# A decoder layer with its self-attention fed from a host-transposed x, the normalisation folded in later, and a new instruction order

## The chip, the core and the metric

The kernel runs on one core of one Trainium2 chip. The metric is the device time of one execution in microseconds; the engines named are PE (TensorE), DVE (VectorE), ACT (ScalarE), POOL (GpSimd) and SP (SyncE, which here only issues DMAs).

## The reference

One decoder layer on 8 items of 512 tokens and 256 channels, in f32:

```python
x = x + attn(layernorm(x))          # one head of 128: q, k, v = xn @ w_q, xn @ w_k, xn @ w_v
                                    # softmax(q k^T / sqrt(128)) v, times head_dim_mask, @ w_o
x = x + xattn(layernorm(x), ctx)    # relu(xn W^T + b), relu(ctx W^T + b), masked softmax, times ctx
x = x + ffn(layernorm(x))           # ternary weights, activations rounded to 8 bits per token:
                                    # silu(gate) * up, 1024 wide, then down to 256
```

`layernorm` subtracts the mean over the 256 channels and divides by sqrt(var + 1e-5); it has no weights.

## The kernel before

The work is cut into streams. Stream A is the self-attention of an item, E projects the item's context, B is the cross-attention, C the feed-forward part, W prepares the weights. A step is written `A.S2/3`: stream A, step S2, item 3. Five lists written out in the file (`PE_ORDER`, `ACT_ORDER`, `DVE_ORDER`, `POOL_ORDER`, `SP_ORDER`) fix what each engine runs, one entry after the other; semaphores join the engines. An engine whose next entry isn't ready waits, and everything behind it in its list waits too. All DMAs are issued by SP, in the order of its list.

Products are made in f32r from a high and a low part: `product3` (L821 to L823) issues high by high, low by high, high by low. So each operand needs a high part (ACT copies it with rounding) and a low part (a subtraction on DVE, or on POOL).

Stream A of one item, as it stands: `bn` and `ag` (DVE) give mean and variance of each token, `rs` (POOL, L537 and L539) gives 1/std, `sh` (DVE, L1040) gives -mean/std, and `norm` (ACT, L632) writes the normalised rows `a_xn`. XT0 and XT1 transpose them on PE (L847), eight 128x128 blocks in all. ACT rounds the two halves from PSUM into `a_xT_hi` (L645), DVE subtracts into `a_xT_lo` (L1139). V, Q and K are products of 6 matmuls each, 512 columns wide. ACT copies V out (L649), PE transposes it (VT). S0 to S3 are the four row blocks of the scores, 3 matmuls each; DVE takes each one's row maximum (L1144), ACT the exponential straight from PSUM (L657) into one of two halves of `a_p`; P0 to P3 transpose that on PE (L878). H is the product with v, 12 matmuls, and Y0, Y1 the product with `w_o`, 12 matmuls half as wide, which DVE adds to x.

Item 0 alone uses five PSUM banks for stream A; later items alternate between two. The start holds the first items' loads (SP), the splitting of all weights, and W.sum0 to W.sum5 (DVE, L1220), the sums of the feed-forward weights, of which sum2 and sum3 need `w_up`. E.YP0 and E.YP1 of an item are 6 matmuls each.

The stretch from the warm-up matmuls (L995) to item 1 reads in `PE_ORDER`:

```python
    A.XT0/0 A.XT1/0 E.YP0/0 A.V/0 A.Q/0 A.K/0 A.VT/0 E.YP1/0 A.S0/0 A.S1/0 A.S2/0 A.S3/0 A.P0/0 A.P1/0 A.P2/0
    A.P3/0 E.YP0/1 A.H/0 E.YP1/1 A.Y0/0 A.Y1/0 W.total/0 A.XT0/1 A.XT1/1 E.YP0/2 A.V/1 A.Q/1 A.K/1 B.XT0/0
```

Of the kernel before, what the change touches and what calls it, by code (L numbers as in the profile page):

```python
# [36 lines left out]
A_LO = ["XT0", "XT1", "Q", "K", "VT", "P0", "P1", "P2", "P3", "H"]  # L37
# [151 lines left out]
    S.hT3/6 S.xqT3/7 S.hT0/7 S.store/6 S.hT1/7 S.hT2/7 S.hT3/7 S.store/7""".split()  # L189


def decoder_layer(nc, x, ctx, ctx_t, mask, head_mask, w_qkv, w_o, W, b, w_gate, w_up, w_down, out):
    B, S = mask.shape
    D, DH = w_o.shape[1], w_o.shape[0]
    F = w_gate.shape[2]
# [1128 lines left out]
```

## Time and profile before

| | us |
|---|---|
| median of 3 runs | 399.21 |
| lowest, highest | 398.03, 399.86 |
| the profiled execution, its own time | 398.97 |
| its span (first to last instruction) | 397.2 |

The profiled execution lies 0.24 us under the median, and 1.8 us lie outside its span. The profile says how long each engine was busy and what ended its idle times. In a row of a timeline the first number is the start, the second the duration; matmuls are pipelined, so their starts tell their pace, not their durations.

### The profile page before, as it was taken

How to read it: one execution, taken by the hardware profiler on the slowest of the kernel's cores; microseconds unless marked ns; L12 is line 12 of the kernel's file. 1: busy time of each engine (PE TensorE's matmuls, PEld its weight loads, DVE VectorE, ACT ScalarE, POOL GpSimd, SP SyncE). 2: the span in 40 equal slices, each digit the busy share in tenths (PEclk: the TensorE clock that was granted, in tenths of full speed). 3: DMA queues.
4: the chain of work that ended last, by engine and by line, in shares of the span. 5: the costliest groups of instructions: out<-in, count | busy, mean ns of one | idle time of the engine just before them, and what ended most of it. 6: DMA issues, size and time to landing. Idle time of an engine off the chain costs nothing.

```text
span 397.2 us, 7277 instructions
## 1 busy us (share of the span) xinstructions
PE 372.9 (94%) x2158; PEld 289.4 (73%) x2158; DVE 332.4 (84%) x908; ACT 328.1 (83%) x611; POOL 270.3 (68%) x398
## 2 busy tenths in 40 slices
PE   5889989999999999999999999999999999999673
PEld 5666667877797688777787778877887788578332
DVE  2999745958998799888998599988997989899991
ACT  3696997699979887998797998889989978966861
POOL 3466931298779846998588786888568866974540
PEclk9699999999999999999999999999999999999995
DMA  7951100022133421225241342252203001432364
GB/s 228 414 196 55 54 2 1 9 66 66 29 59 94 144 57 35 60 61 173 33 71 58 94 127 28 41 141 66 49 6 94 14 0 30 121 65 54 101 139 106
DMA packets 50087, 32.18 MB, mean 81 GB/s; under 512 B 43649, under 2 KB 45313, under 8 KB 49665
## 3 DMA queue, kind: packets, MB, share of 16 engines
q1 hardware_dynamic: 50048, 31.73, 30.1%
q8 instruction: 17, 0.28, 0.3%
q14 instruction: 22, 0.17, 0.2%
HBM read 17.04 MB, written 4.19 MB: 53 GB/s over the span
## 4 chain that ended last, share of the span: by engine, by line
PE 49%; DVE 15%; ACT 14%; issue 10%; POOL 7%; DMA 3%; SPq 1%; DVEq 0%; POOLq 0%; ACTq 0%
PE b_bank L821 5%; PE b_bank L823 5%; PE b_bank L822 5%; PE d_bank L990 4%; PE u_bank L981 4%; PE g_bank L981 4%; PE a_bank L821 3%; PE a_bank L823 3%; PE a_bank L822 3%; POOL c_work L547 2%; PE a_bank L878 2%; DVE h_max L1201 2%; PE b_bank L940 2%; PE e_bank L821 2%; DMA hm_i<-in_head_mask 2%
## 5 line engine op out<-in xcount | busy, mean ns | idle before, releaser
L547 POOL TENSOR_TENSOR c_work<-c_work 128x512 f32<-128x512 f32 x48 | 61.9, 1291 | 20.4 <-DVE c_work L1189 13.2
L588 POOL TENSOR_SCALAR c_work<-c_work,h_q 128x1024 f32<-128x1024 f32 x32 | 36.1, 1128 | 19.6 <-DVE h_q L1208 19.6
L990 PE MATMUL d_bank<-downT,c_half 128*128 128x256 bf16 x256 | 34.9, 282 | 9.0 <-DMA c_half<-c_half 5.4
L750 ACT ACTIVATE c_half<-c_work 128x1024 bf16<-128x1024 f32 x32 | 33.8, 1056 | 9.5 <-POOL c_work L588 9.4
L1201 DVE TENSOR_REDUCE h_max<-c_work 128x1 f32<-128x1024 f32 x32 | 38.8, 1212 | 2.4 <-POOL c_work L547 2.1
L740 ACT ACTIVATE c_work<-g_bank,c_tanh_scale 128x512 f32<-128x512 f32 x52 | 36.4, 699 | 4.2 <-PE g_bank L981 3.1
L821 PE MATMUL b_bank<-ctx_hi,b_pT_hi 128*128 128x256 f32 x128 | 38.9, 304 | 0.0
L1189 DVE SCALAR_TENSOR_TENSOR c_work<-c_work,g_bank 128x512 f32<-128x512 f32 x52 | 35.4, 680 | 3.7 <-ACT c_work L740 3.0
L990 PEld LDWEIGHTS d_bank<-downT,c_half 128*128 128x128 bf16 x256 | 24.4, 100 | 19.1 <-DMA c_half<-c_half 8.3
L822 PE MATMUL b_bank<-ctx_lo,b_pT_hi 128*128 128x256 f32 x128 | 36.1, 282 | 0.0
L823 PE MATMUL b_bank<-ctx_hi,b_pT_lo 128*128 128x256 f32 x128 | 36.1, 282 | 0.0
L981 PE MATMUL g_bank<-gateT,xqT 128*128 128x512 bf16 x112 | 33.5, 381 | 1.2 <-ACT c_work L728 0.9
L981 PE MATMUL u_bank<-upT,xqT 128*128 128x512 bf16 x112 | 33.6, 382 | 0.2 <-DMA xqT<-xq 0.2
L743 ACT ACTIVATE c_work<-u_bank 128x512 f32<-128x512 f32 x48 | 29.2, 609 | 4.6 <-PE u_bank L981 2.8
L1144 DVE TENSOR_REDUCE a_nmax<-a_bank 128x1 f32<-128x512 f32 x29 | 19.9, 687 | 14.7 <-PE a_bank L823 14.5
L514 POOL TENSOR_TENSOR yp_lo<-e_relu,yp_hi 128x512 fp32r<-128x512 f32 x16 | 20.7, 1293 | 14.1 <-ACT yp_hi L677 14.1
L821 PE MATMUL b_bank<-yp_hi,xp_hi 128*128 128x512 f32 x64 | 28.4, 444 | 0.0
L686 ACT ACTIVATE b_p<-b_p,b_nmax 128x512 f32<-128x512 f32 x32 | 23.6, 736 | 3.3 <-DVE b_nmax L1169 3.3
L821 PEld LDWEIGHTS b_bank<-ctx_hi,b_pT_hi 128*128 128x128 f32 x128 | 24.3, 190 | 2.0 <-DVE b_pT_lo L1163 0.6
L823 PE MATMUL b_bank<-yp_hi,xp_lo 128*128 128x512 f32 x64 | 25.2, 394 | 0.0
L822 PE MATMUL b_bank<-yp_lo,xp_hi 128*128 128x512 f32 x64 | 25.1, 392 | 0.0
L822 PEld LDWEIGHTS b_bank<-ctx_lo,b_pT_hi 128*128 128x128 f32 x128 | 24.3, 190 | 0.4
(254 smaller groups left out, 1278.4 us busy)
## 6 DMA issues: line engine op xcount, KB each, us to landing
ctxT_raw<-in_ctx_t SPq DMA_DIRECT2D x8, 512.0 KB, 3.9
ctx_raw<-in_ctx SPq DMA_DIRECT2D x8, 512.0 KB, 3.5
x_all<-in_x SPq DMA_DIRECT2D x7, 512.0 KB, 3.8
out<-x_all SPq DMA_DIRECT2D x7, 512.0 KB, 2.6
c_half<-in_w_down SPq DMA_DIRECT2D x1, 1024.0 KB, 7.4
c_work<-in_w_gate SPq DMA_DIRECT2D x1, 1024.0 KB, 10.1
c_work<-in_w_up SPq DMA_DIRECT2D x1, 1024.0 KB, 11.7
x_all<-in_x SPq DMA_DIRECT2D x2, 256.0 KB, 2.8
```

The lines of the kernel that those rows point to most:

```text
L547: pool.tensor_tensor(h[:, t % 2, half * HALF:(half + 1) * HALF], th[:, j % 2, :], up[:, j % 2, :], ALU.mult).then_inc(hs, 1)
L588: pool.tensor_scalar(h[:, t % 2, :], h[:, t % 2, :], h_q[:, t:t + 1], ROUND, ALU.mult, ALU.add).then_inc(h_rounds, 1)
L740: act.activation(th[:, j % 2, :], gu_bank("g", j, n), ACT.Tanh, scale=c_tanh_scale[:, j // 2:j // 2 + 1]).then_inc(tanhs, 1)
L743: act.activation(up[:, j % 2, :], gu_bank("u", j, n), ACT.Copy).then_inc(ups, 1)
L750: act.activation(h_q8[:, t % 2, :], h[:, t % 2, :], ACT.Copy, bias=-ROUND).then_inc(hqs, 1)
L821: pe.matmul(dst, l_hi, r_hi, start=first, stop=False)
L822: pe.matmul(dst, l_hi, r_lo, start=False, stop=False)
L823: return pe.matmul(dst, l_lo, r_hi, start=False, stop=last)
L981: mm = pe.matmul(dst, xqT[:, t * DC + c, :], w[:, c, cols], start=c == 0, stop=c == DC - 1)
L990: mm = pe.matmul(d_bank[:, 0:D], h_T[:, t % 2, f, :], downT[:, f, :], start=f == 0, stop=f == FC - 1)
L1189: dve.scalar_tensor_tensor(th[:, j % 2, :], th[:, j % 2, :], 1.0, gu_bank("g", j, n), ALU.add, ALU.mult).then_inc(gates, 1)
L1201: dve.tensor_reduce(h_max[:, one], h[:, t % 2, :], AX.X, ALU.max, apply_absolute_value=True).then_inc(h_maxes, 1)
```

## The change

x is loaded twice: as rows, for the residual and the statistics, and as `x_t`, transposed on the host (`a_xT_raw`, 512 KB an item). Attention works on the raw x. Taking the mean off the channels of x is the same as taking the mean over the 256 channels off each column of the weights, so `w_qkv` is centred once (W.colsum on PE, W.centre on DVE). 1/std is a factor of a token: of a column of v and of a column of the scores it enters by a row `r_bc` of 512 values, the same in all partitions; of a row of the scores it enters as a scalar. `r_bc` is made by two DMAs an item: S.rw stores 1/std to a row in DRAM, S.rb reads it back broadcast to 128 partitions. So that the row comes out in order, tokens are numbered 4 to a partition, and q is written with its columns re-ordered.

XT0, XT1, `norm`, `sh` and the copy of V are gone. In their place stand `xT0`, `xT1` (ACT rounds from SBUF; the low part is made by POOL, for item 0 by DVE), the product of V with `r_bc` on DVE, and for each S one DVE operation that multiplies, writes `a_p` and takes the maximum, with a small one behind it that negates the maximum. ACT's exponential now reads `a_p`. The bank of an S is free again once DVE has read it; before, once ACT had taken the exponential. As DVE now writes `a_p`, S2 and S3 wait on DVE for P0 and P1.

All five lists are new.

```diff
+            def load_xT(n):
+                if n > 1:
+                    sp.wait_ge(xT_loaded, (n - 1) * 16)
+                    sp.wait_ge(xT_split, DC * (n - 1))
+                else:
+                    sp.wait_ge(xT0_split, DC)
+                sp.dma_start(a_xT_raw[:, :, :], x_t[:, n]).then_inc(xT_loaded, 16)
...
+            def store_r(n):
+                sp.wait_ge(a_rstds, 4 * n + 4)
...
+                sp.dma_start(r_rows[n, :].rearrange("(p t) -> p t", t=T), a_rstd[:, n % 2, :]).then_inc(r_stored, 16)
...
+            def load_r(n):
+                sp.wait_ge(r_stored, 16 * n + 16)
...
+                    sp.wait_ge(a_maxed, T * n)
+                sp.dma_start(r_bc[:, :], r_rows[n, :].partition_broadcast(P)).then_inc(r_loaded, 16)
...
+            def xT_rest(c, n):
+                pool.wait_ge(xT_his, DC * n + c + 1)
+                pool.tensor_tensor(a_xT_lo[:, c, :], a_xT_raw[:, c, :], f32(a_xT_hi[:, c, :]), ALU.subtract).then_inc(xT_split, 1)
...
-            def copy_v(n):
-                act.wait_ge(a_filled, a_rank("V", n))
-                act.activation(vT[:, :], a_bank("V", n)[:, :], ACT.Copy).then_inc(vT_copied, 1)
...
+            def round_xT(c, n):
...
+                act.activation(a_xT_hi[:, c, :], a_xT_raw[:, c, :], ACT.Copy).then_inc(xT_his, 1)
...
-                act.wait_ge(a_maxed, T * n + t + 1)
...
-                act.activation(a_p[:, t % 2, :], a_bank(f"S{t}", n)[:, :], ACT.Exp,
+                act.wait_ge(a_nmaxes, T * n + t + 1)
+                act.activation(a_p[:, t % 2, :], a_p[:, t % 2, :], ACT.Exp,
...
-                    for t in range(T):
-                        if c == 0 and t % 2 == 0:
-                            pe.wait_ge(a_xns, 2 * n + t // 2 + 1)
-                        mm = pe.transpose(dst[:, t * P:(t + 1) * P], a_xn[:, t, c * P:(c + 1) * P], ident[:, :])
...
+                if name == "colsum":
+                    pe.wait_ge(qkvo_loaded, 16)
+                    for c in range(DC):
+                        mm = pe.matmul(b1_bank[:, 0:3 * DH], ones[:, :], wqkv_raw[:, c, :, :].rearrange("p w d -> p (w d)"),
+                                       start=c == 0, stop=c == DC - 1)
...
-                    dve.tensor_reduce(a_nmax[:, t:t + 1], src[:, :], AX.X, ALU.max, negate=True).then_inc(a_maxed, 1)
+                    if t > 1:
+                        dve.wait_ge(a_filled, a_rank(f"P{t - 2}", n))
...
+                    dve.tensor_tensor_reduce(a_p[:, t % 2, :], src[:, :], r_bc[:, :], a_rstd[:, n % 2, t:t + 1], MASKED, ALU.mult, ALU.max,
+                                             a_max[:, t:t + 1]).then_inc(a_maxed, 1)
+                    dve.wait_ge(a_maxed, k)
+                    dve.tensor_scalar(a_nmax[:, t:t + 1], a_max[:, t:t + 1], -1.0, None, ALU.mult).then_inc(a_nmaxes, 1)
+                elif step == "V":
+                    dve.wait_ge(a_filled, a_rank(step, n))
+                    dve.wait_ge(r_loaded, 16 * n + 16)
+                    dve.tensor_tensor(vT[:, :], src[:, :], r_bc[:, :], ALU.mult).then_inc(vT_copied, 1)
...
+            def centre_qkv():
+                dve.wait_ge(qkv_sums, 1)
+                for c in range(DC):
...
+                    last = dve.scalar_tensor_tensor(raw, b1_bank[:, 0:3 * DH], -1.0 / D, raw, ALU.mult, ALU.add)
+                last.then_inc(qkv_centred, 1)
```

Of `PE_ORDER` the piece that answers to the one above now reads:

```diff
+    W.colsum/0 A.Q/0 A.K/0 A.V/0 A.VT/0 A.S0/0 A.S1/0 A.S2/0 A.S3/0 A.P0/0 A.P1/0 E.YP0/0 A.P2/0 A.P3/0 E.YP1/0
+    W.total/0 A.H/0 E.YP0/1 A.Y0/0 A.Y1/0 E.YP1/1 A.Q/1 A.K/1 A.V/1 A.VT/1 B.XT0/0 B.XT1/0 A.S0/1 A.S1/1 B.XP0/0
```

SP's list at the start, of before; `in_w_qkv` and `in_w_o` go to `b_p`, `in_w_up` and `in_w_gate` to `c_work`:

```order
L452 DMA x_all<-in_x 128x512 x2
L409 DMA ctxT_raw<-in_ctx_t 128x1024
L456 DMA b_p<-in_w_qkv 128x768
L458 DMA b_p<-in_w_o 128x256
L460 DMA bias<-in_b 128x2
L462 DMA hm_i<-in_head_mask 128x1
L454 DMA xqT<-in_W 128x512
L465 DMA c_half<-in_w_down 128x2048
L397 DMA x_all<-in_x 128x1024
L465 DMA c_work<-in_w_gate 128x2048
L416 DMA mask_u<-in_mask 128x512
L465 DMA c_work<-in_w_up 128x2048
```

And of the changed kernel, the piece from the fifth load on; `r_rows` is the row in DRAM, `r_bc` its broadcast:

```order
L406 DMA x_all<-in_x 128x1024
L498 DMA c_work<-in_w_gate 128x2048
L439 DMA ctxT_raw<-in_ctx_t 128x1024
L412 DMA ctx_raw<-in_ctx 128x1024
L498 DMA c_half<-in_w_down 128x2048
L446 DMA mask_u<-in_mask 128x512
L495 DMA hm_i<-in_head_mask 128x1
L498 DMA c_work<-in_w_up 128x2048
L426 DMA r_rows<-a_rstd 128x4
L406 DMA x_all<-in_x 128x1024
L420 DMA a_xT_raw<-in_x_t 128x1024
L433 DMA r_bc<-r_rows 128x512
```

Ahead of this piece stand x (two halves), `w_qkv`, the bias, `x_t` (two halves), W and `w_o`. What moved: `x_t` of item 0 and the contexts now stand in front of `w_up`, and the store of 1/std stands behind `w_up`, its broadcast read two loads of 512 KB further on.

DVE's list of before from the splitting of `w_o` (W.wo, L1242 to L1245) to W.sum2; L1251 splits W, L1220 is a W.sum:

```order
L1242 CAST hm_f<-hm_i 128x1
L1243 TENSOR_SCALAR b_p<-b_p,hm_f 128x256
L1244 CAST wo_hi<-b_p 128x256
L1245 TENSOR_TENSOR wo_lo<-b_p,wo_hi 128x256
L1247 TENSOR_TENSOR wqkv_lo<-b_p,wqkv_hi 128x768
L1251 TENSOR_TENSOR wt_lo<-xqT,wt_hi 128x512
L1139 TENSOR_TENSOR a_xT_lo<-a_bank,a_xT_hi 128x512 x2
L1028 BN_STATS a_bn<-x_all 128x6 x4
L1035 BN_AGGR a_mv<-a_bn 128x2 x4
L1220 TENSOR_REDUCE w_sum<-c_work 128x1
L1040 TENSOR_SCALAR a_shift<-a_mv,a_rstd 128x1 x2
L1220 TENSOR_REDUCE w_sum<-c_work 128x1 x2
```

And of the changed kernel from W.sum0 on; L1214 is the product of V with `r_bc`, L1323 belongs to W.wo, the splitting of `w_o`, and L1207 with L1210 to the step S:

```order
L1290 TENSOR_REDUCE w_sum<-c_work 128x1 x2
L1188 SCALAR_TENSOR_TENSOR q_lo<-a_bank,q_hi 128x512
L1290 TENSOR_REDUCE w_sum<-c_work 128x1
L1196 TENSOR_TENSOR k_lo<-a_bank,k_hi 128x512
L1214 TENSOR_TENSOR vT<-g_bank,r_bc 128x512
L1322 CAST hm_f<-hm_i 128x1
L1323 TENSOR_SCALAR b_p<-b_p,hm_f 128x256
L1324 CAST wo_hi<-b_p 128x256
L1325 TENSOR_TENSOR wo_lo<-b_p,wo_hi 128x256
L1196 TENSOR_TENSOR v_lo<-u_bank,v_hi 128x512
L1207 ISA a_p,a_max<-d_bank,r_bc,a_rstd 128x512
L1207 ISA a_max 128x1
```

What moved: W.wo and the split of W (L1329) stood ahead of item 0's scores and of everything that waits for a load of `w_up`; now W.wo stands behind the product with `r_bc`, the split of W behind S1. Behind the piece follow S2, S3, P0, P1, three of the six sums, P2, P3, the statistics of items 1 to 3, W.scales and H.

## Rows read from the trace of the kernel before

**Rows 1.** The page: busy us, share of the span and instructions of each engine
```profile
PE 372.9 (94%) x2158; PEld 289.4 (73%) x2158; DVE 332.4 (84%) x908; ACT 328.1 (83%) x611; POOL 270.3 (68%) x398
```

**Rows 2.** Busy by stretch: stretch, length, PE, PEld, DVE, ACT, POOL, clock, DMA share, GB/s
```profile
10.00:20.00 10.00, 8.53 (x29) 6.50 (x30) 9.51 (x20) 6.75 (x13) 4.23 (x6) 0.66 1.01 415
20.00:30.00 10.00, 8.75 (x47) 6.65 (x46) 9.40 (x15) 9.49 (x20) 6.00 (x4) 1.00 0.54 189
30.00:40.00 10.00, 9.05 (x48) 6.84 (x47) 9.47 (x34) 6.81 (x13) 6.32 (x7) 1.00 0.19 55
50.00:60.00 10.00, 8.62 (x46) 7.00 (x45) 4.83 (x10) 10.00 (x19) 2.82 (x3) 1.00 0.01 2
100.00:140.00 40.00, 39.96 (x246) 32.05 (x245) 35.09 (x93) 35.71 (x68) 32.50 (x45) 1.00 0.34 88
```

**Rows 3.** What PE waited for: us in total, times, longest us
```profile
PE d_bank L990 <- DMA c_half<-c_half: 5.4, 4, 2.7
PE a_bank L847 <- ACT a_xn L632: 3.9, 2, 3.6
```

**Rows 4.** Timeline of PE: start us, us, engine, line, operation, count, idle before
```profile
20.80 0.60 PE L863 MATMUL a_bank<-ident,vT 128*128 128x128 f32 x4
...
21.70 0.40 PE L823 MATMUL e_bank<-ctxT_hi,wt_lo 128*128 128x512 f32 x1
21.94 0.39 PE L821 MATMUL e_bank<-ctxT_hi,wt_hi 128*128 128x512 f32 x1
...
37.50 1.44 PE L847 MATMUL a_bank<-ident,a_xn 128*128 128x128 f32 x8 [0.17 <-DVE x_all L1151]
...
246.25 1.03 PE L847 MATMUL a_bank<-ident,a_xn 128*128 128x128 f32 x8
247.12 0.59 PE L981 MATMUL u_bank<-upT,xqT 128*128 128x512 bf16 x2
```

**Rows 5.** Groups of instructions: line, engine, operation, count, busy us, mean ns, idle
```profile
L847 PE MATMUL a_bank<-ident,a_xn 128*128 128x128 f32 x64 | 10.5, 296 | 4.2 <-ACT a_xn L632 3.9 <-DVE x_all L1151 0.2
...
L1169 DVE CUSTOM_DVE_ANT_0 b_p<-b_bank,mask_add 128x512 f32<-128x512 f32 x32 | 21.9, 683 | 0.9 <-PE b_bank L823 0.8
...
L1028 DVE BATCH_NORM_STATS2 a_bn<-x_all 128x6 f32<-128x256 f32 x32 | 11.6, 412 | 3.4 <-DMA x_all<-in_x 3.4
...
L1139 DVE TENSOR_TENSOR a_xT_lo<-a_bank,a_xT_hi 128x512 fp32r<-128x512 f32 x16 | 10.4, 681 | 0.2 <-ACT a_xT_hi L645 0.2
...
L1040 DVE TENSOR_SCALAR a_shift<-a_mv,a_rstd 128x1 f32<-128x1 f32 x32 | 5.2, 206 | 2.2 <-POOL a_rstd L539 2.2
...
L632 ACT ACTIVATE a_xn<-x_all,a_shift,a_rstd 128x256 f32<-128x256 f32 x32 | 17.1, 594 | 1.9 <-DVE a_shift L1040 1.9
...
L514 POOL TENSOR_TENSOR yp_lo<-e_relu,yp_hi 128x512 fp32r<-128x512 f32 x16 | 20.7, 1293 | 14.1 <-ACT yp_hi L677 14.1
```

**Rows 6.** Timelines of POOL (first row) and DVE, 5 to 30 us
```profile
8.90 2.35 POOL L510 TENSOR_TENSOR ctxT_lo<-ctxT_raw,ctxT_hi 128x1024 fp32r<-128x1024 f32 x1 [1.74 <-ACT ctxT_hi L707]
...
9.80 1.59 DVE L1243 TENSOR_SCALAR b_p<-b_p,hm_f 128x256 f32<-128x256 f32 x1
11.43 0.29 DVE L1244 CAST wo_hi<-b_p 128x256 fp32r<-128x256 f32 x1
11.76 0.43 DVE L1245 TENSOR_TENSOR wo_lo<-b_p,wo_hi 128x256 fp32r<-128x256 f32 x1
...
19.36 1.22 DVE L1220 TENSOR_REDUCE w_sum<-c_work 128x1 f32<-128x1024 f32 x1 [0.42 <-DMA c_work<-in_w_up]
...
25.75 0.68 DVE L1144 TENSOR_REDUCE a_nmax<-d_bank 128x1 f32<-128x512 f32 x1
26.35 1.21 DVE L1220 TENSOR_REDUCE w_sum<-c_half 128x1 f32<-128x1024 f32 x1
```

**Rows 7.** DMA issues: out<-in, queue, count, KB each, median us to landing
```profile
c_work<-in_w_up SPq DMA_DIRECT2D x1, 1024.0 KB, 11.7
...
mask_u<-in_mask SPq DMA_DIRECT2D x8, 64.0 KB, 3.2
```

More of the change, by code:

```diff
@@ L192, in decoder_layer @@
-def decoder_layer(nc, x, ctx, ctx_t, mask, head_mask, w_qkv, w_o, W, b, w_gate, w_up, w_down, out):
+    W.colsum/0 A.Q/0 A.K/0 A.V/0 A.VT/0 A.S0/0 A.S1/0 A.S2/0 A.S3/0 A.P0/0 A.P1/0 E.YP0/0 A.P2/0 A.P3/0 E.YP1/0
+    W.total/0 A.H/0 E.YP0/1 A.Y0/0 A.Y1/0 E.YP1/1 A.Q/1 A.K/1 A.V/1 A.VT/1 B.XT0/0 B.XT1/0 A.S0/1 A.S1/1 B.XP0/0
+    B.XP1/0 A.P0/1 A.S2/1 E.YP0/2 A.P1/1 A.S3/1 B.S0/0 B.S1/0 A.P2/1 A.P3/1 B.P0/0 B.S2/0 A.H/1 B.P1/0 B.O0/0
+    A.Y0/1 B.S3/0 B.P2/0 A.Y1/1 A.Q/2 B.O1/0 B.P3/0 A.K/2 B.O2/0 B.O3/0 A.V/2 B.XT0/1 B.XT1/1 E.YP1/2 A.VT/2
@@ L193, in decoder_layer @@
+def decoder_layer(nc, x, x_t, ctx, ctx_t, mask, head_mask, w_qkv, w_o, W, b, w_gate, w_up, w_down, out):
     B, S = mask.shape
@@ L1029, in a_norm @@
                     last.then_inc(a_stats, 1)
-                elif part == "ag":
+                else:
                     dve.wait_ge(a_stats, k)
                     if n > 0:
-                        dve.wait_ge(a_shifts, k - 2)
+                        dve.wait_ge(a_rstds, 2 * (k - 2))
                     for t in pair(half):
@@ L1036, in a_norm, with xT0_rest @@
                     last.then_inc(a_mvs, 1)
-                else:
-                    dve.wait_ge(a_rstds, 2 * k)
-                    for t in pair(half):
-                        last = dve.tensor_scalar(a_shift[:, t:t + 1], a_mv[:, t, 0:1], a_rstd[:, t:t + 1], -1.0, ALU.mult, ALU.mult)
-                    last.then_inc(a_shifts, 1)
+            def xT0_rest(c):
+                dve.wait_ge(xT_his, c + 1)
+                dve.tensor_tensor(a_xT_lo[:, c, :], a_xT_raw[:, c, :], f32(a_xT_hi[:, c, :]), ALU.subtract).then_inc(xT0_split, 1)
             def b_norm(part, half, n):
@@ L1258, in step @@
                     else:
-                        {"split": split_qkvo, "lo": split_W, "scales": prep_scales}[name]()
+                        {"centre": centre_qkv, "split": split_qkv, "wo": split_wo, "lo": split_W, "scales": prep_scales}[name]()
+                elif name[:2] == "xT":
+                    xT0_rest(int(name[2]))
                 elif name[:2] in ("ag", "sh") and stream == "C" and n == LAST:
@@ L1300 @@
     laid_out = {
-        "x": tokens(x),
+        "x": own_tokens(x),
+        "x_t": x.reshape(*x.shape[:2], -1, P).transpose(3, 0, 2, 1),
         "ctx": tokens(ctx),
```

449 lines of the change are left out of this document (243 added, 206 removed).

## The prediction

> **What bounds the kernel now.** I read the page's busy shares first. PE is busy for 372.9 of 397.2 us, DVE 84%, ACT 83%, POOL 68% [rows 1]. The reader is to see one engine nearly full and none far below it. Then the table of stretches, since a share is a mean: from 100 to 140 PE has 39.96 of 40 us, with DVE at 35.09, ACT at 35.71 and POOL at 32.50 [rows 2]. There PE is the bound. In the first 40 us it isn't: PE has 8.53, 8.75 and 9.05 of each 10 while DVE has 9.51, 9.40 and 9.47, so DVE is the fuller one; and DMA is saturated from 10 to 20 (share 1.01, 415 GB/s) [rows 2]. Last the list of what PE waited for: 5.4 us for the transposed h, at the end of the kernel, and 3.9 us for the normalised x, nearly all of it in one wait of 3.6 at the start [rows 3]. So the change must be judged twice: where PE is full, and in the start.
>
> **PE in the full part.** 64 transposes go [rows 5]. Their mean duration of 296 ns is not their price, since they overlap: eight of them start at 246.25 and the next work at 247.12, so 0.11 us each [rows 4]. For items 1 to 7 that is 56 x 0.11 = 6.2 us off PE. As PE is full there, I count all of it. It is the only gain that reaches the end.
>
> **The other engines in the full part.** DVE loses 16 subtractions (10.4 us) and 32 shifts (5.2 us) [rows 5]. It gains 8 products with `r_bc` and 32 small negations, and the 32 row maxima become multiply-and-maximum operations. A PSUM-reading operation of 128x512 takes 0.68 to 0.69 whichever it is: L1139 681 ns, L1169, which is the same kind as the new one, 683 ns [rows 5], the old maximum 0.68 [rows 6]. So the maxima cost the same, the products 8 x 0.68 = 5.5, the negations 32 x 0.21 = 6.6 at the price of L1040 [rows 5], and 32 reads of an accumulator some 0.1 each, 3: together 15.1 against 15.6. DVE stands as it was. ACT loses the norms, 17.1 us [rows 5], and the copies of V; that is hidden by PE. POOL gains 14 subtractions at 1.293 us [rows 5], 18 us in all, 2.6 an item: from 32.5 to about 35 in a stretch of 40 [rows 2]. That is hidden by PE too, as long as POOL's latencies don't grow; if that cover goes, 2.6 us an item are the most it can cost. The pair of DMAs for 1/std holds SP: when S.rb stands right behind S.rw, SP stands still until the row is stored, about the 3.2 us of a small load [rows 7], and the transposes of h stand behind it. PE waited for those only at the end [rows 3], so I count nothing.
>
> **The start.** Here the order decides. First the loads. The store of 1/std stands behind `w_up`. Before, `w_up` landed at 19.4: DVE's sum waited for it until 19.36 [rows 6]. By the shapes in the two lists (128x1024 in f32 are 512 KB; the mask is 64 KB) before has 5,441 KB up to and with `w_up`, the new list 6,465 KB, since `ctx` and the 512 KB of `x_t` now stand in front of it. 1,024 KB at 415 GB/s [rows 2] are 2.5 us: `w_up` lands at 21.9, and the row of 1/std hardly before, because a small DMA doesn't overtake: `w_up` needed 11.7 us although it is only 1,024 KB, which alone is 2.5 us [rows 7]. The read of `r_bc` is issued then, behind 1,024 KB more and with 256 KB of its own: 3.1 us, 25.0. An idle queue would give 21.9 + 3.2 = 25.1 [rows 7], so both ways lead to the same time. Until 25.0 DVE stands at the product of V, and behind it stands all that it does for item 0.
>
> Then the work behind that wait. DVE's list from A.V/0 up to H of item 0 has: 8 operations of 128x512, 0.60 apart (25.75 to 26.35) [rows 6], 4.8; 4 steps S at 0.60 + 0.1 + 0.21, 3.6; W.wo, from 9.80 to 12.19 in before [rows 6] and a small cast, 2.5; three sums of 1.21 that overlap by 0.1 [rows 6], 3.3; 6 statistics at 0.41 [rows 5], 2.5; 21 small ones (aggregations, a reciprocal, W.scales), which I put at 0.12 each, under L1040's 0.206 because they overlap, 2.5. Together 19.2. So H's low part is ready at 44.2. Y0 and Y1 (12 half-wide matmuls, 1.4) and E.YP1/1 (6 at 0.24 [rows 4], 1.4) follow, and A.Q/1 starts at 47.0. Before, the same place in the work is 37.50 plus eight transposes, 38.4 [rows 4]: by then both kernels have done four YP steps and item 0's attention. **The delay is 8.6 us.**
>
> Its bounds. If DVE were no limit, PE would need from 25.7 on: 48 matmuls at 0.24, 20 transposes at 0.11, 12 half-wide at 0.12, 15.1 us [rows 4], so A.Q/1 at 40.8 and a delay of 2.4. From above, some 2 us of waits of ACT and POOL between DVE's operations, 10.6. I take 8.6, because DVE's operations in this stretch stood back to back in before (9.40 and 9.47 of 10 [rows 2]) and work that used to lie before 24 us (W.wo, the split of W, W.sum3) is now behind 25. The new matmuls of W.colsum fall while PE has nothing else, and item 0's own transposes are within the delay as counted.
>
> W.wo has a price that hangs on its neighbour. Its multiplication took 1.59 us, while a cast of the same shape took 0.29, and POOL's L510 ran from 8.90 to 11.25 beside it [rows 6]. In the new order POOL's two `a_xT_lo` of item 1 fall beside it again, so I keep 2.5. The Trainium skill (SBUF — State Buffer, SBUF: two separate sides) says that DVE and GpSimd arbitrate for one pair of ports, "an exclusive lock, not a bandwidth split". By that rule, W.wo without POOL beside it would be 1.2, the delay 7.3 and the whole 400.1; the rule and the row agree on the collision, and what it leaves open is only whether POOL is there.
>
> **The sum**, against the profiled execution's own time: 398.97 - 6.2 + 8.6 = 401.4. That execution lies 0.24 below the median, so 401.6, which I round to **401.5 us**, 0.6% slower. A measurement of this kernel tells about 0.5%, 2.0 us, from no change.
>
> **Rivals.**
> - *The delay is made good later; faster.* Between 50 and 60 PE had only 8.62 and ACT all of 10 us [rows 2]. ACT loses four norms an item, 2.1 us; for items 1 and 2, 4.2, and PE's idle 1.4 of that stretch could be filled. 401.4 - 5.6 = 395.8. For it: DVE has room there (4.83 of 10). Against it: PE can only work off what it waits for, and it waits little after 60. It decides once the place of A.S0/2 in the new trace is less than 4 us late. 0.27.
> - *The row of 1/std comes sooner; no change.* If a small DMA does overtake the loads, V's product still waits for W.sum2, which needs `w_up`: 21.9 + 1.1 + 0.6 for K, 23.6 rather than 25.0, and with W.wo free of POOL another 1.3 less. 401.4 - 1.4 - 1.3 = 398.7. Against it: 11.7 us for `w_up`. 0.16.
> - *POOL and SP lose as well; clearly slower.* If the 2.6 us that POOL gets more an item show on the path at only a quarter, seven items cost 4.5: 405.9. For it: POOL is at 81% in the full part. 0.17.
> - *The forecast*, start late, transposes saved: 0.40, its own range 399.5 to 404.
>
> **The numbers.** The forecast's own 0.40 splits at 401.2, the bound of 0.5%, into 0.25 above and 0.15 below. Slower: 0.25 + 0.17 = 0.42. Within 0.5%: 0.15 + 0.13 of the second rival + 0.02 of the first, 0.30. Faster: 0.25 + 0.03, 0.28. The range takes the delay's lower bound, 398.97 - 6.2 + 2.4 = 395.2, at one end, and the third rival at the other: 395 to 406.
>
> **What would show it.** In the new trace: V's product on DVE ends an idle time near 25 with a DMA as releaser; A.VT/0 near 25.8 against 20.80; H of item 0 around 41 to 45 on PE; A.Q/1 near 47. In the full part eight transposes fewer per item, PE still at 39.9 of 40, POOL near 35. It is wrong if `r_bc` lands before 22, if DVE idles between 25 and 44, if PE idles visibly more than before between 60 and 340, or if PE's waits at the end, 5.4 for h [rows 3], change by more than 2 us, which the new order could do and the trace of before can't tell.

## The result, and the profile after

The changed kernel takes **405.21 us** (median of four runs, 403.0 to 406.9) against 399.19 for the kernel before: a ratio of 1.015, 95% interval 1.0086 to 1.0215, 6.0 us slower. The profiled execution was its fastest run: 403.0 us with a span of 401.2. It is 4.0 us above the profiled execution of before, where the forecast was 2.4.

Two rows of the page of the changed kernel, its span and the busy share of each engine, to be read beside [rows 1]:

```profile
span 401.2 us, 7242 instructions
...
PE 367.7 (92%) x2098; PEld 283.6 (71%) x2098; DVE 331.2 (83%) x936; ACT 311.4 (78%) x571; POOL 287.3 (72%) x412
```

PE has 5.2 us less, ACT 16.7 less, POOL 17.0 more, DVE the same within 1.2: near the counts of the prediction (6.2 off PE, 17.1 and the copies of V off ACT, 18 on POOL, DVE as it was). The table of stretches (columns as in [rows 2]) says where the time went:

```profile
10.00:20.00 10.00, 6.01 (x18) 4.48 (x18) 5.31 (x8) 1.20 (x2) 0.00 (x0) 0.83 0.85 342
20.00:30.00 10.00, 3.27 (x10) 2.79 (x11) 5.72 (x9) 3.21 (x5) 2.99 (x3) 0.60 0.52 192
30.00:40.00 10.00, 8.01 (x37) 6.00 (x36) 9.69 (x25) 8.04 (x17) 6.42 (x7) 0.88 0.59 177
40.00:50.00 10.00, 7.35 (x36) 5.88 (x37) 9.36 (x31) 6.00 (x8) 8.54 (x6) 1.00 0.40 104
...
100.00:140.00 40.00, 40.00 (x236) 31.86 (x236) 35.91 (x104) 34.15 (x66) 33.38 (x48) 1.00 0.27 62
```

From 10 to 30 us PE has 9.3 us of work where it had 17.3 [rows 2], and DVE, which was nearly full, 11.0 of 20. From 100 on PE is full as before. The rest is in four timelines of the changed kernel. First DVE (start us, us, engine, line, operation, idle before it and who ended it):

```profile
22.17 1.22 DVE L1290 TENSOR_REDUCE w_sum<-c_work 128x1 f32<-128x1024 f32 x1 [6.05 <-DMA c_work<-in_w_up]
...
25.99 0.69 DVE L1214 TENSOR_TENSOR vT<-g_bank,r_bc 128x512 f32<-128x512 f32 x1 [2.00 <-DMA r_bc<-r_rows]
26.78 1.26 DVE L1323 TENSOR_SCALAR b_p<-b_p,hm_f 128x256 f32<-128x256 f32 x1
...
41.99 1.25 DVE L1297 TENSOR_TENSOR w_mean<-w_half 128x3 f32<-128x3 f32 x1
43.28 1.23 DVE L1298 TENSOR_SCALAR w_mean<-w_mean 128x3 f32<-128x3 f32 x1
44.54 0.18 DVE L1299 RECIPROCAL w_inv<-w_mean 128x3 f32<-128x3 f32 x1
...
46.36 0.67 DVE L1196 TENSOR_TENSOR hT_lo<-g_bank,hT_hi 128x512 fp32r<-128x512 f32 x1
```

Then SP's queue, with the store of 1/std and its broadcast; POOL beside DVE's two slow tiny operations; and PE:

```profile
9.15 0.56 SPq L426 DMA_DIRECT2D r_rows<-a_rstd  x1
...
22.68 0.33 SPq L433 DMA_DIRECT2D r_bc<-r_rows  x1
```

```profile
40.82 2.40 POOL L553 TENSOR_TENSOR ctxT_lo<-ctxT_raw,ctxT_hi 128x1024 fp32r<-128x1024 f32 x1
43.18 1.31 POOL L557 TENSOR_TENSOR yp_lo<-e_relu,yp_hi 128x512 fp32r<-128x512 f32 x1
```

```profile
26.73 1.12 PE L915 MATMUL u_bank<-ident,vT 128*128 128x128 f32 x4 [8.89 <-DVE vT L1214]
...
28.50 0.63 PE L881 MATMUL d_bank<-k_hi,q_lo 128*128 128x512 f32 x1
28.93 0.63 PE L879 MATMUL a_bank<-k_hi,q_hi 128*128 128x512 f32 x1
...
47.14 0.36 PE L879 MATMUL u_bank<-wo_hi,hT_hi 128*128 128x256 f32 x1 [2.19 <-DVE hT_lo L1196]
...
50.03 0.39 PE L879 MATMUL a_bank<-a_xT_hi,wqkv_hi 128*128 128x512 f32 x1
```

The reader is to see one chain. The store of 1/std, 2 KB, was issued at 9.15, but SP, which waits for that store to land, could issue the broadcast only at 22.68, half a us after `w_up` had landed. So V's product stands at 25.99, PE idles 8.89 us in one piece, and all of item 0 follows late. The last row is A.Q/1, the first work of item 1. In the kernel before, the same place in the work is the end of item 1's eight transposes, 38.4 ([rows 4], as in the prediction); its first product of item 1 itself starts at 40.78, behind one product of E. In the changed kernel the place is 50.03. **11.6 us are lost up to there.** From there to the end of the span before needed 358.8 us and the changed kernel 351.2. **7.6 us are given back.** The difference is the 4.0. What the 7.6 are made of stands in the table of stretches, taken from that place to the end, before and then changed:

```profile
38.40:397.20 358.80, 342.19 (x2018) 264.82 (x2018) 302.78 (x833) 303.02 (x567) 251.49 (x369) 0.99 0.27 65
```

```profile
50.03:401.20 351.17, 336.76 (x1967) 259.05 (x1965) 296.80 (x854) 289.33 (x536) 266.57 (x383) 0.99 0.33 78
```

PE is busy for 5.4 us less and idle for 2.2 us less (14.4 and not 16.6).

This pair, where A.Q/1 starts and what is left from there, is what the experiments are measured by.

### The profile page after: what moved, and what is told of

Its sections match the earlier page's. It is cut to its first block, busy times and chain, and to the rows that moved or that the text cites. A ratio compares the mean times of both kernels' runs of the same rounds, so it can differ in the third digit from the quotient of the medians.

```text
span 401.2 us, 7242 instructions
## 1 busy us (share of the span) xinstructions
PE 367.7 (92%) x2098; PEld 283.6 (71%) x2098; DVE 331.2 (83%) x936; ACT 311.4 (78%) x571; POOL 287.3 (72%) x412
## 4 chain that ended last, share of the span: by engine, by line
PE 55%; POOL 14%; DVE 9%; issue 7%; DMA 7%; ACT 6%; SPq 2%; POOLq 0%; ACTq 0%; DVEq 0%
PE b_bank L879 7%; PE b_bank L881 7%; PE b_bank L880 7%; PE a_bank L879 4%; PE a_bank L881 4%; PE a_bank L880 4%; PE g_bank L1033 4%; PE u_bank L1033 3%; DMA r_rows<-a_rstd 3%; PE d_bank L1042 3%; POOL c_work L601 3%; PE b_bank L992 3%; PE a_bank L926 2%; POOL c_work L642 2%; DMA c_half<-c_half 2%
## 5 line engine op out<-in xcount | busy, mean ns | idle before, releaser
L549 POOL TENSOR_TENSOR a_xT_lo<-a_xT_raw,a_xT_hi 128x512 fp32r<-128x512 f32 x14 | 17.9, 1294 | 18.1 <-ACT a_xT_hi L715 18.1
L1207 DVE CUSTOM_DVE_ANT_0 a_p<-a_bank,r_bc,a_rstd 128x512 f32<-128x512 f32 x30 | 22.4, 746 | 8.3 <-PE a_bank L881 8.1
L879 PE MATMUL b_bank<-yp_hi,xp_hi 128*128 128x512 f32 x64 | 27.4, 428 | 0.2
L545 POOL TENSOR_TENSOR ctx_lo<-ctx_raw,ctx_hi 128x1024 fp32r<-128x1024 f32 x8 | 19.2, 2398 | 10.6 <-ACT ctx_hi L762 10.6
L719 ACT ACTIVATE a_p<-a_p,a_nmax 128x512 f32<-128x512 f32 x32 | 23.7, 745 | 3.6 <-DVE a_nmax L1210 3.6
```

The lines of the kernel that those rows point to most:

```text
L879: pe.matmul(dst, l_hi, r_hi, start=first, stop=False)
```

## The experiments

| kernel | median us | ratio to before | A.Q/1 at | from there on |
|---|---|---|---|---|
| changed kernel | 405.2 | 1.015 (1.009 to 1.022) | 50.03 | 351.2 |
| row early | 407.2 | 1.021 (1.018 to 1.023) | 54.05 | 352.0 |
| row early, path clear | 402.6 | 1.009 (1.006 to 1.012) | 47.79 | 352.0 |
| DVE cleared | 405.6 | 1.016 (1.014 to 1.019) | 51.58 | 351.9 |
| both | 399.5 | 1.003 (1.000 to 1.006) | 43.91 | 353.2 |
| transposes back | 408.8 | 1.026 (1.022 to 1.029) | 53.16 | 355.3 |
| POOL twice | 420.1 | 1.053 (1.049 to 1.056) | 51.45 | 364.2 |
| scales later | 409.3 | 1.028 (1.025 to 1.031) | 48.95 | 357.6 |
| start reordered | 412.4 | 1.034 (1.031 to 1.037) | 50.11 | 360.4 |
| POOL a quarter | 404.9 | 1.014 (1.010 to 1.018) | 53.57 | 350.7 |
| ACT twice | 410.5 | 1.028 (1.025 to 1.032) | 53.01 | 356.1 |
| second order | 407.3 | 1.021 (1.017 to 1.024) | 42.95 | 361.8 |
| third order | **397.4** | **0.9976 (0.9958 to 0.9995)** | 38.43 | 355.8 |

The last two columns are those of the profiled run. The fourth is not sharp: between runs with the same lists up to there it differs by up to 3.5 us, and 1.5 of these are PE's clock (see "DVE cleared"). All medians of before in these comparisons lie between 398.8 and 399.2.

### Is it the row of 1/std?

**Row early.** SP's list alone is changed:

```diff
-S.x/1 W.gate/0 S.ctxT/0 S.ctx/0 W.down/0 S.mask/0 W.hm/0 W.up/0 S.rw/0 S.x/2 S.xT/1 S.rb/0
+S.x/1 S.rw/0 W.gate/0 S.ctxT/0 S.rb/0 S.ctx/0 W.down/0 S.mask/0 W.hm/0 W.up/0 S.x/2 S.xT/1
```

> The changed kernel, with only the two DMAs of item 0's 1/std row moved forward in SP's list: the store right behind x of item 1, the broadcast read right behind the context. Theory 1 (the row waits behind the loads of w_up and w_down, and that is what starts item 0's scores late): the row lands near 14.5 instead of 26, but V's product still stands behind W.sum2 on DVE, which needs w_up near 22; so V's product moves from 26.0 to about 24.5, PE's wait at A.VT/0 shrinks by 1.5, and the time falls by 1.5 us, to about 403.5 by the median. Rival (the path of item 0 doesn't matter, the loss is spread over the items): nothing moves by more than 0.5 us.

It was slower than the changed kernel. In DVE's timeline the row isn't waited for any more, but the sum that stands ahead of the product comes 3.2 us later:

```profile
25.34 1.22 DVE L1290 TENSOR_REDUCE w_sum<-c_work 128x1 f32<-128x1024 f32 x1 [7.00 <-DMA c_work<-in_w_up]
...
27.07 0.68 DVE L1214 TENSOR_TENSOR vT<-g_bank,r_bc 128x512 f32<-128x512 f32 x1
```

SP stands still until 1/std is there and again until it is stored, and every load behind it is issued later. `w_up` was issued at 13.28 and not at 8.65. In the changed kernel DVE had waited only 2.00 us for the row, so more than that was not to be had from the row alone, and SP's wait took it away again. A.Q/1 moved by 4.0 us and V's product by 1.1; 1.5 of the difference is PE's clock, granted at 0.50 from 50 to 52 us, as told under "DVE cleared".

**Row early, path clear.** The same, with DVE's W.sum2, which needs `w_up`, behind A.S1/0, and ACT's and POOL's rounding of item 1's x behind A.exp1/0 and E.ctxT/0:

```diff
 DVE
-A.Q/0 W.sum2/0 A.K/0 A.V/0 W.wo/0 A.VT/0 A.S0/0 A.S1/0 W.lo/0
+A.Q/0 A.K/0 A.V/0 W.wo/0 A.VT/0 A.S0/0 A.S1/0 W.sum2/0 W.lo/0
```

> As e1_row_early, and the steps that stand in front of item 0's path and wait for late loads are moved behind it: W.sum2 on DVE (needs w_up) behind A.S1/0, the rounding of item 1's x on ACT behind A.exp1/0, and its low part on POOL behind E.ctxT/0. Theory 1: V's product near 18.5 instead of 26.0, A.VT/0 near 19.5, A.Q/1 near 43 instead of 50.0, and the time 7 us lower, about 398 by the median. Rival A (DVE's own list, not the wait, sets A.Q/1): A.Q/1 moves by less than 3 us, time near 403. Rival B (the loss is spread over the items): time as the changed kernel's.

V's product came at 18.62, 7.4 us earlier. A.Q/1 came only 2.2 us earlier, and the median fell by 2.6, which is the size that rival A had. From V's product to the end of H's low part it now took 26.2 us and not 21.0. DVE's next step wanted a load that hadn't come either:

```profile
22.74 0.15 DVE L1320 CAST hm_f<-hm_i 128x1 f32<-128x1 int32 x1 [3.44 <-DMA hm_i<-in_head_mask]
22.93 1.62 DVE L1321 TENSOR_SCALAR b_p<-b_p,hm_f 128x256 f32<-128x256 f32 x1
```

**DVE cleared.** The loads as in the changed kernel, but W.wo and W.lo ahead of A.Q/0 on DVE, and W.hi behind W.qkv on ACT, so that less stands behind the wait:

```diff
 DVE
-W.split/0 A.bn1/1 W.sum0/0 W.sum1/0 A.Q/0 W.sum2/0 A.K/0 A.V/0 W.wo/0 A.VT/0 A.S0/0 A.S1/0 W.lo/0 W.sum3/0
+W.split/0 A.bn1/1 W.sum0/0 W.sum1/0 A.Q/0 W.wo/0 W.lo/0 W.sum2/0 A.K/0 A.V/0 A.VT/0 A.S0/0 A.S1/0 W.sum3/0
```

> The changed kernel with the loads as they are; DVE's W.wo and W.lo are moved from behind the wait for the row to ahead of A.Q/0, where DVE is idle (and ACT's rounding of W behind that of w_qkv). Theory 1 with DVE as the limit behind the wait: 2.2 and 1.1 us less work between V's product and H, so A.Q/1 at 46.7 instead of 50.0 and the time 3.3 us lower, 402. Rival (PE or ACT sets the pace behind the wait): under 1 us.

No gain, though W.wo's multiplication took 0.35 us there (POOL idle beside it) and no longer 1.26. V's product came at 26.61, 0.6 later, and H's low part ended at 47.05, as in the changed kernel (47.03). Of the 3.3 us taken out of DVE's list behind the wait, 2.1 came back as idle time (1.84 for the high part of V, which ACT makes, 0.28 for the scores, at PE's lower clock) and 0.5 because the first small product of W.scales stood longer beside POOL (1.76 us and not 1.25). So the step "DVE's list behind the wait is the whole delay" is only half right: with W.wo and W.lo out of the list, the others' chain takes most of its place.

A.Q/1 is 1.5 us later all the same, from the same start of Y0 (47.15 and 47.14). The stretch from 48 to 50 us, here and then in the changed kernel; the granted clock stands behind POOL's share of it (0.50 and 1.00):

```profile
48.00:50.00 2.00, 2.00 (x9) 1.90 (x9) 1.37 (x4) 2.00 (x2) 1.96 (x2) 0.50 0.00 0
```

```profile
48.00:50.00 2.00, 2.00 (x13) 1.76 (x12) 1.88 (x5) 2.00 (x2) 1.98 (x2) 1.00 0.03 8
```

Here the clock fell behind PE's wait of 2.2 us for H's low part, and the products of E followed each other at 0.43 us. It did so too in "row early", "transposes back", "POOL a quarter" and "ACT twice" (4.4 us from Y0 to A.Q/1), and not in "row early, path clear", "POOL twice" and the changed kernel (2.9 us), behind waits of 1.8 to 2.2 us. What decides it, these runs don't show.

**Both**, with the broadcast behind the load of W.gate, and one product of E in PE's wait behind A.V/0; ACT's rounding of item 1's x stands behind its first two exponentials. Two of the lists:

```diff
 SP
+S.x/1 S.ctxT/0 W.hm/0 S.rw/0 W.gate/0 S.rb/0 S.ctx/0 W.down/0 S.mask/0 W.up/0
 PE
-A.V/0 A.VT/0
+A.V/0 E.YP0/0 A.VT/0
```

> Both together: the row early, the context and the head mask ahead of the feed-forward weights, W.lo, W.wo, the rounding of the context and E.YP0/0 in the time that engines were idle, W.sum2 and item 1's x behind item 0's path. Theory 1: V's product near 18.5, A.Q/1 near 41, so that nearly the whole start is given back; with the 7.6 us that the rest of the program is shorter than before, 395 to 396, under the kernel before. Rival B (the loss is spread): no better than 403.

V's product at 19.25, A.Q/1 at 43.91 (41 expected), and the time not to be told from before's: 399.5, between the 395 to 396 forecast and the rival's 403. What stood in the way next is one row of PE, where the third exp was late, as ACT stood at item 1's x and DVE at two sums of the weights:

```profile
30.98 1.94 PE L924 MATMUL a_bank<-ident,a_p 128*128 128x128 f32 x8 [5.65 <-ACT a_p L717]
```

### Where do the 7.6 us come from?

**Transposes back.** Eight transposes of the identity ahead of A.Q of items 1 to 7:

```diff
+                    if step == "Q" and n > 0:
+                        for _ in range(2 * T):
+                            pe.transpose(dst[:, 0:P], ident[:, :], ident[:, :])
```

> The changed kernel with eight transposes of the identity put ahead of A.Q of each of items 1 to 7, as many as the change took away there, with no copies and no engine behind them. If what the change gives back behind its start is PE's own time, as the forecast has it, these 56 cost 56 x 0.11 = 6.2 us: profiled 409 us beside the 403.0 of the changed kernel, A.Q/1 as before near 50. The rival: the 7.6 us that the changed kernel gained behind 50 us came from waits or from the lighter DVE list; then PE has some slack and the same transposes cost less than 4 us, under 407.

```profile
53.16 1.04 PE L908 MATMUL a_bank<-ident 128*128 128x128 f32 x8
53.95 0.47 PE L879 MATMUL a_bank<-a_xT_hi,wqkv_hi 128*128 128x512 f32 x1
```

By the median 3.6 us more, and from A.Q/1 on 355.3 against 351.2, 4.1 more. That lies between the two expectations. From A.Q/1 on PE is busy for 341.9 us, 5.1 more than the 336.8 of the changed kernel, and idle for 1.0 less. So the 56 cost PE 5.1 us of work (0.09 each, where 0.11 was forecast), and 1.0 of it fell into waits.

**ACT twice.** ACT's rounding of the transposed x is done twice in items 1 to 7, 14 x 0.61 = 8.6 us, about half of what the change took from ACT:

```diff
+                    act.activation(a_xT_hi[:, c, :], a_xT_raw[:, c, :], ACT.Copy).then_inc(twice, 1)
+                    act.wait_ge(twice, DC * (n - 1) + c + 1)
                 act.activation(a_xT_hi[:, c, :], a_xT_raw[:, c, :], ACT.Copy).then_inc(xT_his, 1)
```

> The changed kernel with ACT's rounding of the transposed x done twice in items 1 to 7: 14 more of 0.61 us, 8.6 us of ACT, half of the 16.7 us of ACT that the change took away. The transposes put back gave a price of 3.4 to 5.5 us of the 7.6 that the changed kernel gains behind its start. If the rest of that gain comes from ACT's shorter list, this run loses 2 to 4 us behind A.Q/1 (354 to 355 us from there to the end). The rival, that ACT has slack and the gain is PE's alone: 351 to 352 from A.Q/1 to the end, and a total as the changed kernel's.

4.9 us more from A.Q/1 on, nearly all of it waits: of those 356.1 us PE is busy for 335.7, and in "POOL a quarter", whose trace lacks as many matmul records (29), for 335.1 of 350.7. So ACT isn't hidden by PE when its work grows. That its shorter list is what took the 2.2 us off PE's waits is likely from this, and not shown: the order is new as well. PE's busy time between 60 and 100 us, in the run with ACT's work doubled and in the changed kernel:

```profile
60.00:100.00 40.00, 37.09 (x209) 30.51 (x208) 27.79 (x84) 33.13 (x64) 21.33 (x31) 1.00 0.16 47
```

```profile
60.00:100.00 40.00, 39.60 (x227) 32.62 (x225) 27.77 (x86) 33.22 (x67) 22.33 (x33) 1.00 0.17 49
```

The extra work also makes the high part of x itself later, and this run can't tell that from the load on ACT.

**POOL twice and POOL a quarter.** POOL's low part of x is computed twice in items 1 to 7 (+18 us), and then for the first 128 of the 512 positions only, which leaves the rest of that tile as it was:

```diff
-                pool.tensor_tensor(a_xT_lo[:, c, :], a_xT_raw[:, c, :], f32(a_xT_hi[:, c, :]), ALU.subtract).then_inc(xT_split, 1)
+                pool.tensor_tensor(a_xT_lo[:, c, :P], a_xT_raw[:, c, :P], f32(a_xT_hi[:, c, :P]), ALU.subtract).then_inc(xT_split, 1)
```

> The changed kernel with POOL's low part of the transposed x (two of 1.29 us for an item) computed twice in items 1 to 7: 14 more of 1.29 us, 18 us of POOL. If POOL has slack in the full part (33.4 to 35.0 us of 40), the only price is at the start, where the pair of item 1 ends 2.6 us later beside DVE's list: 403 to 406 us. The rival, that POOL sets the pace and the new order suffers from it: 410 us or more, and PE's waits for POOL's low parts of xp and yp grow.

> The changed kernel with POOL's low part of the transposed x cut to the first 128 of 512 positions in items 1 to 7 (the rest keeps what an earlier item left, so the output is another): 14 operations of 1.29 us become about 0.4, some 12 us less POOL. When they were doubled, 18 us more of POOL cost 12 to 13 us behind A.Q/1 (364.2 us from there to the end beside 351.2). If POOL sets the pace already as it stands, the same price works the other way: 8 us less, some 395 us. If PE is what is full (39.9 of 40 us) and POOL only took over when its work was doubled, taking work from it gives at most 2 us: 401 to 405.

More work on POOL cost 13.0 us for its 18, as the rival had it; less work gave 0.5. PE's busy time from 100 to 340, POOL twice first, then POOL a quarter, then the changed kernel:

```profile
100.00:340.00 240.00, 229.94 (x1335) 179.02 (x1333) 200.46 (x578) 197.12 (x376) 205.51 (x273) 1.00 0.33 80
```

```profile
100.00:340.00 240.00, 238.35 (x1383) 188.12 (x1405) 211.04 (x614) 205.68 (x392) 193.32 (x278) 1.00 0.33 81
```

```profile
100.00:340.00 240.00, 239.36 (x1411) 187.88 (x1411) 211.41 (x616) 204.97 (x389) 200.47 (x278) 1.00 0.33 79
```

(The quarter's trace lacks 29 matmul records, which is most of its 1.0 us under the changed kernel.) What PE waited for in the whole of "POOL twice", where the changed kernel has none of the first two rows and 1.0 of the last two:

```profile
PE u_bank L1036 <- ACT c_work L808: 4.6, 3, 2.7
...
PE b_bank L882 <- POOL xp_lo L565: 2.2, 2, 1.6
PE u_bank L1036 <- DMA xqT<-xq: 2.0, 1, 2.0
PE g_bank L1036 <- DMA xqT<-xq: 1.9, 2, 1.0
```

ACT stood 5.0 us for POOL there (L808 waits for L604), and `xq` is POOL's too, so these waits go back to POOL. As it stands POOL costs nothing measurable, at a share of 84%, and what is added in this place is paid at 0.7 us for each. Its share says how much it works, not how soon another engine wants the result. Doubling also makes each low part of x 1.3 us later, and the run can't tell that from the load.

### Can the start be had back?

**Scales later.** In DVE's list W.scales and A.bn0/3 stand behind A.Y1/0 in place of ahead of A.H/0:

```diff
-W.scales/0 A.bn0/3 A.H/0 A.bn1/3 A.Y0/0 A.Y1/0
+A.H/0 A.bn1/3 A.Y0/0 A.Y1/0 W.scales/0 A.bn0/3
```

> The changed kernel with one move in DVE's list: the weights' scales and the first statistics of item 3 stand behind A.Y1/0, not ahead of A.H/0. In the changed kernel the scales held DVE 3.9 us, 2.2 of them in two tiny operations that ran beside POOL's subtractions, and the low part of H stood at 46.36 though its high part was done at 44.1. If DVE's list there is on the path, the low part comes at 44.2, A.Q/1 at 47.9 and not 50.0, and the total falls by 2.1 us, to 401 beside 403.0 (median near 403). The rival: what is lost at the start is set by other things (the rounding of the weights for the FFN that hangs on the scales) and the total does not move or grows.

The near effect came, A.Q/1 at 48.95, in a run whose `w_up` landed at 23.8, and the scales' first operation took 0.16 us. The far effect was larger. PE waits 5 us behind A.Q/1, since ACT stands at the signs of the weights, ahead of the high part of Q:

```profile
56.93 0.67 PE L878 MATMUL a_bank<-a_xT_hi,wqkv_hi 128*128 128x512 f32 x1 [5.04 <-DVE q_lo L1187]
```

```profile
52.54 2.19 ACT L816 ACTIVATE gateT<-c_work,neg_round 128x1024 bf16<-128x1024 f32 x2 [5.24 <-POOL c_work L648]
```

**Start reordered.** This starts from the lists of "both", with the two sums behind all score maxima and ACT's rounding of item 1's x behind item 0's P (the 5.65 us wait falls to 2.19), other places for the products of E, and the scales late too. DVE's part:

```diff
 DVE
-A.S0/0 A.S1/0 W.sum2/0 W.sum3/0 A.S2/0 A.S3/0
+A.S0/0 A.S1/0 A.S2/0 A.S3/0 W.sum2/0 W.sum3/0
...
-W.scales/0 A.bn0/3 A.H/0 A.bn1/3 A.Y0/0 A.Y1/0
+A.H/0 A.Y0/0 A.Y1/0 W.scales/0 A.bn0/3 A.bn1/3
```

> The same instructions as the changed kernel, with the lists around item 0 in another order: the row stored and broadcast early with the loads of W.gate behind it, the low parts of wo and W early, the sums of W_up behind the four score maxima, ACT's rounding of item 1's x and of ctx behind item 0's P, the scales behind A.Y1/0, and each product of E moved to where PE waited (after V, after H, after Y1). In the run with the first half of this, PE waited 5.65 us for the third exp and A.Q/1 stood at 43.9. If the loss of the change is only the order at the start and the gain behind it (7.6 us) stays, A.Q/1 comes near 40 and the total is 351 + 40 + 1.8 = 393 us, 394 by the median. The rival: the gain is used up because the loads (w_up at 24 us, the x of item 1 near 26) or ACT's list hold item 1 in any order: 397 to 400, no better than before.

A miss of 18 us by the median, and the slowest order of all, outside the rival's range too. A.Q/1 isn't earlier than in the changed kernel, and 360.4 us follow it. PE's product with the weights' sums, put ahead of H, waited 3.79 us for them; its products of E, which were to fill waits, waited 1.99 for POOL and 1.45 for ACT.

**Second order.** The scales right behind H's low part, all low parts of P ahead of the sums of W_down, ACT's Q of item 1 ahead of its second sign:

```diff
 DVE
+A.S3/0 W.sum2/0 W.sum3/0 A.ag0/1 A.ag1/1 A.P0/0 A.P1/0 A.P2/0 A.P3/0 W.sum4/0 A.inv/0 W.sum5/0 A.H/0 W.scales/0 A.Y0/0 A.Y1/0
 SP
+S.x/2 S.xT/1 S.ctxT/1 S.x/3 S.mask/1 S.rw/1 S.rb/1 S.xT/2 S.mask/2 S.ctx/1 S.ctxT/2
```

> The start reordered once more, from what the run with the first reordering showed: the scales of the weights must not come later than 37 us, since POOL's rounding, ACT's signs and with them the high part of Q of item 1 stand behind them. Here the scales stand behind the low part of H, which comes earlier (all four score maxima ahead of the sums of W_up, P of all four blocks ahead of the sums of W_down), ACT takes Q of item 1 ahead of its second sign, and the load of ctxT of item 1 no longer stands behind the wait of SP for item 1's x. By the durations of the rows H starts near 31.5, the low part of H near 35, A.Q/1 near 40, and with 352 us behind it the span is 392 and the time 394 us. The rival: what is gained at the start comes back as waits between 40 and 80 us, since the weights' rounding and item 1's x and r row come no earlier: 397 to 400.

A.Q/1 at 42.95 (40 expected), and 407.3 us, above both expectations. Behind it comes one wait of 7.92 us, which can be read backwards through four timelines, PE, ACT, SP and POOL:

```profile
57.34 0.69 PE L961 MATMUL b_bank<-ident,b_xn 128*128 128x128 f32 x2 [7.92 <-ACT b_xn L688]
```

```profile
54.20 1.06 ACT L767 ACTIVATE ctxT_hi<-ctxT_raw 128x1024 fp32r<-128x1024 f32 x1 [7.53 <-DMA ctxT_raw<-in_ctx_t]
```

```profile
49.46 0.33 SPq L410 DMA_DIRECT2D ctx_raw<-in_ctx  x1
49.88 0.38 SPq L437 DMA_DIRECT2D ctxT_raw<-in_ctx_t  x1
```

```profile
47.03 2.36 POOL L543 TENSOR_TENSOR ctx_lo<-ctx_raw,ctx_hi 128x1024 fp32r<-128x1024 f32 x1
```

**Third order.** Four moves against what those rows show:

```diff
 SP
-S.mask/2 S.ctx/1 S.ctxT/2
+S.ctxT/2 S.mask/2 S.ctx/1
 POOL
-A.rs0/2 B.ctx/0
+B.ctx/0 A.rs0/2
 PE
-E.YP1/1 A.Q/1
+A.Q/1 E.YP1/1
 DVE
-W.sum2/0 W.sum3/0 A.ag0/1 A.ag1/1 A.P0/0 A.P1/0 A.P2/0 A.P3/0
+W.sum2/0 A.ag0/1 A.ag1/1 A.P0/0 A.P1/0 A.P2/0 A.P3/0 W.sum3/0
```

> The second reordering with four moves more. There A.Q/1 stood at 42.95 (50.03 in the changed kernel), but PE then waited 7.92 us for the transposes of item 0's second attention: ACT stood 7.53 us at the ctxT of item 2, whose load SP had issued only at 49.88, behind the load of ctx of item 1, which waited for POOL's rounding of ctx (47.03, done 49.4). Now the load of ctxT of item 2 stands ahead of the mask of item 2, POOL's rounding of ctx ahead of its third rstd, the second product of E of item 1 behind A.Q/1 (PE waited 1.45 us for it), and the fourth sum of the weights behind the low parts of P (PE waited 2.03 us for these). If the cost of the change is only this start, A.Q/1 comes near 40.5 with one product of E left, and with 351 to 352 us behind it the span is 392 to 393 and the time 394 us, under both kernels. The rival, which each run so far has borne out, is that the next late step takes the place of the one removed: 397 to 401.

```profile
38.43 0.50 PE L877 MATMUL a_bank<-a_xT_hi,wqkv_hi 128*128 128x512 f32 x1 [0.34 <-DVE x_all L1219]
```

397.4 us by the median of 12: 0.24% under the kernel before (interval 0.05% to 0.42%) and 7.8 us under the changed one, with that kernel's instructions. A.Q/1 stands at the 38.4 of before, with one product of E still behind it (1.4 us), and 355.8 us follow. The forecast of 394 was missed by 3.4, and the time lies in the rival's range, 397 to 401. 355.8 are 4.6 more than the changed kernel's 351.2: 1.4 are that product, and 2.3 are longer waits of PE between 45 and 58 us, five of 0.15 to 1.49 that add up to 3.9 where the changed kernel had three with 1.6. The last 0.9 isn't placed.

## Why the prediction was right, and what in it was off

The median, 405.21, lies in the range and on the side given the highest chance, above the forecast's own 399.5 to 404, and 3.7 us from the predicted time. The mechanism held, a late start and a gain behind it; both sizes were low. That the range reached as far as 406 is luck: its upper end is the third rival's price for POOL, which the quarter run doesn't bear out, and not a price for the start, where the time was lost. By the forecast's own terms the range would have ended at 404.

- **What bounds the kernel.** Right. PE is busy for 239.4 of 240 us from 100 to 340 in both.
- **Loads.** `w_up` at 21.9 forecast, 22.17 measured. That the small store of 1/std doesn't overtake the loads was right: issued 9.15, done shortly before 22.68; so with the head mask, 0.5 KB, which needed 11.4 us from its issue at 8.16. `r_bc` was forecast for 25.0 and came at 25.99: the broadcast took 3.3 us from its issue (3.1 forecast) and was issued 0.8 later.
- **The work behind the wait.** 19.2 us forecast, 21.0 measured (25.99 to 47.03 as H's low part ends). 2.2 of it are the two tiny operations of W.scales, which lasted 1.25 and 1.23 us and not 0.16. Both ended with the POOL operation beside them, at 43.24 and 44.51. The Trainium skill's rule of the shared port pair (SBUF — State Buffer, SBUF: two separate sides) was used in the prediction on W.wo alone; the place where it cost most, on operations that the sum had at 0.12 us each, was missed. The trace agrees with the rule here, and on W.wo too: 1.26 us beside POOL, 0.35 with POOL idle ("DVE cleared").
- **The delay.** 8.6 forecast, 11.6 measured, above the upper bound of 10.6. 1.0 is the broadcast, 1.8 the list, 0.2 the rest. The step that failed is the bound: it took 2 us for all that might stand between DVE's operations, and nothing for a landing that varies or for PE's clock.
- **The median.** The profiled run was lucky. In four later kernels with the same loads and nearly the same lists up to there (transposes back, POOL twice, POOL a quarter, ACT twice) `w_up` landed at 22.8 to 24.1, Y0 began at 48.6 to 49.1 and not at 47.1, and A.Q/1 at 51.5 to 53.6; in three of the four the fallen clock makes 1.5 of it. With 351.2 us behind it the median of the changed kernel would mean, as an estimate, A.Q/1 near 52.1 and a delay of 13.7. The kernel before spreads less: all its runs lie between 398.0 and 400.2. How its loads varied no trace shows.
- **The gain.** 6.2 forecast for the transposes, 7.6 measured in all: 5.4 less work of PE and 2.2 less waiting. The sum counts eight transposes twice. The place 38.4 lies behind item 1's own, so taking them off is in the delay of 8.6 already; behind it only 48 go, 48 x 0.11 = 5.3, which PE's 5.4 bear out. The sum should have read 398.97 - 5.3 + 8.6 = 402.3. The 2.2 us of shorter waits had no term. ACT's lighter list, costed at nothing as "hidden by PE", may be their cause.
- **DVE and POOL in the full part.** Right as costed, nothing. The new multiply-and-maximum takes 746 ns, not 683; from 100 to 340 PE is as full as before with it. POOL came to 33.4 to 35.0 of 40; "hidden by PE too" is right by the quarter run, and POOL twice shows how little more it would take.
- **The rivals.** Made good later: no more than the 2.2 us of shorter waits. Its sign was ill chosen: A.S0/2 came at 90.98 against 87.42, 3.6 late and so under the 4 that it named, but the first product of item 1's cross-attention (B.XP0/1) came at 91.89 against 83.10, so the order between them had changed and one step's place tells little. The row comes sooner: the run with it early shows `w_up` as the next bound, as the rival said (23.6 forecast), but SP's own wait made it 27.07. POOL and SP lose as well: its time, 405.9, is the nearest to the measured median, by chance; the quarter run gives POOL 0.5 us. The waits for the transposed h at the end grew from 5.4 [rows 3] to 7.2 us, within the 2 us allowed.

What stays open: what took the 2.2 us off PE's waits, ACT's lighter list or the new order. A run with ACT's old work at its old place wasn't tried.

## What to carry to other kernels

When a change puts a short wait in front of an engine with a fixed list, price the whole list behind it and then the next late item: here V's product came 7.4 us earlier and A.Q/1 2.2, until sums, scales, loads and ACT's work for item 1 had been moved as well. A cover of 16% on an engine is no slack by itself: POOL gave 0.5 us when relieved of 11 and took 0.7 us for each one added. A change whose instructions are right and whose place in the lists is not looks like a slow change; here it went from 1.5% slower to 0.2% faster by order alone. The kernel before had no such search for its order, so the 0.2% isn't the worth of the change. And two places in two traces compare work only if the same work lies behind both: here eight transposes were counted twice.
